# GNN and mixture layer on one core: edge products as two fp32r products of weighted rows, in lots of four edge tiles

## The reference

```python
# _layernorm: no gain, no bias, eps 1e-5
support = _layernorm(x) @ W
x = x + segment_sum(support[src] * edge_weight[:, None], dst, 12500) + b
# the experts, on h = _layernorm(x); one sample, so one routing for all tokens
w = softmax(mean(h) @ Wr + br)                 # capped by capacity, softmax again, top 2, softmax
y = sum over the two chosen e: w_e * (gelu(h @ W1[e] + b1[e]) @ W2[e] + b2[e])
x = x + layernorm(y + h, gamma, beta)
```

## Time and profile before

| | us |
|---|---|
| median of three runs | 2384.93 |
| the profiled execution: its own time | 2382.08 |
| the profiled execution: span | 2380.3 |
| PE busy / PEld busy | 2210.0 / 1729.8 |
| DVE busy | 1025.3 |
| ACT busy | 1193.3 |
| POOL busy | 1516.3 |
| first gather, last gather (start) | 11.27, 1973.68 |

### The profile page before, as it was taken

How to read it: one execution, slowest core, us unless ns; L and a number is a source line. 1 busy time by engine, 2 the same in 40 slices (tenths; PEclk the granted TensorE clock), 3 DMA queues, 4 the chain that set the end, 5 groups by cost and what they waited for, 6 DMA issues and landing times. The chain is left out here.

```text
span 2380.3 us, 41661 instructions
## 1 busy us (share of the span) xinstructions
PE 2210.0 (93%) x9949; PEld 1729.8 (73%) x9950; DVE 1025.3 (43%) x2952; ACT 1193.3 (50%) x3202; POOL 1516.3 (64%) x1594
## 2 busy tenths in 40 slices
PE   2488999899999999999999999999998999999998
PEld 1366777677776767777777777777776777999998
DVE  7893233232332233232332322232222235899989
ACT  3577666665655555544534343322324125565664
POOL 6777777777777777777777777777777771000100
PEclk9999999999999999999999999999999999999999
DMA  9955667666666655566656656556566554242431
GB/s 369 336 168 157 205 202 241 187 189 180 180 187 181 181 176 175 178 179 197 186 178 180 189 179 187 175 182 190 169 194 172 186 161 141 95 140 95 136 98 54
DMA packets 226740, 425.79 MB, mean 179 GB/s; under 512 B 36675, under 2 KB 134774, under 8 KB 226600
## 3 DMA queue, kind: packets, MB, share of 16 engines
q0 software_dynamic: 75008, 204.90, 29.5%
q1 hardware_dynamic: 151160, 217.12, 28.0%
q10 hardware_dynamic: 432, 2.40, 0.3%
HBM read 341.53 MB, written 82.75 MB: 178 GB/s over the span
## 5 line engine op out<-in xcount | busy, mean ns | idle before, releaser
L588 POOL DMA_INDIRECT G<-xr_d,SRC x1467 | 1391.8, 949 | 447.0 <-issue 298.6
L1072 DVE TENSOR_SCALAR OH<-CST,DL,WR 128x128 f32<-128x128 f32 x1563 | 567.4, 370 | 1272.3 <-PE ps L1463 1151.0
L1463 PE MATMUL ps<-G,OH 128*128 x3126 | 739.8, 389 | 78.6 <-DVE OH L1072 57.8
L1463 PEld LDWEIGHTS ps<-G,OH 128*128 128x128 f32 x3126 | 597.0, 194 | 224.1 <-issue 143.0
L1446 PE MATMUL ps<-W2u,H 128*128 128x256 f32 x1920 | 430.9, 382 | 6.9 <-issue 6.3
L1435 PE MATMUL ps<-YU,W1u 128*128 128x512 f32 (+1 forms) x1024 | 426.1, 568 | 9.6 <-ACT H L767 8.4
L1446 PEld LDWEIGHTS ps<-W2u,H 128*128 128x128 f32 x1920 | 363.1, 191 | 69.8 <-issue 20.9
L1435 PEld LDWEIGHTS ps<-YU,W1u 128*128 128x128 f32 x1024 | 194.8, 191 | 206.1 <-issue 184.7
L775 ACT ACTIVATE YE<-ps 128x512 f32<-128x512 f32 (+1 forms) x128 | 72.6, 569 | 442.3 <-PE ps L1446 442.1
L767 ACT ACTIVATE H<-ps,b1a 128x512 f32<-128x512 f32 (+1 forms) x256 | 168.5, 660 | 225.9 <-PE ps L1435 225.6
L602 POOL TENSOR_TENSOR ZR<-ZV,mhalf 128x4 f32<-128x4 f32 (+1 forms) x24 | 30.5, 1272 | 348.6 <-DVE ZV L1256 348.6
(11 more groups left out here) (221 smaller groups left out, 2302.1 us busy)
## 6 DMA issues: line engine op xcount, KB each, us to landing
W1u<-in_W SPq DMA_DIRECT2D x64, 512.0 KB
W2u<-in_W SPq DMA_DIRECT2D x64, 512.0 KB, 4.7
y_d<-YE SPq DMA_DIRECT2D x56, 512.0 KB, 5.7
G<-xr_d,SRC POOLq DMA_INDIRECT x1467
x_d<-X SPq DMA_DIRECT2D x98, 128.0 KB
yt_d<-YT SPq DMA_DIRECT2D x98, 128.0 KB
XR<-in_x SPq DMA_DIRECT2D x97, 128.0 KB, 3.1
XL<-x_d SPq DMA_DIRECT2D x24, 512.0 KB, 4.9
```

What stands on the lines that cost most here:

```text
L588: e.indirect_dma_start(out=G[0:rows(s), held(s), :], out_offset=None, in_=x if s < FRESH else xr_d, in_offset=bass.IndirectOffsetOnAxis(ap ...
L1072: e.tensor_scalar(OH[:, s % OHR, :], iota, DL[:, s:s + 1], WR[:, s + 1:s + 2], ALU.is_equal, ALU.mult).then_inc(s_oh, 1)
L1463: e.matmul(ps[:, 0, 0:D], OH[:, r, :], Gf[:, bass.ds(g + r * D, D)], start=False, stop=True, skip_group_check=True).then_inc(s_main, 1)
```

## The change

The edge product is no longer fp32 with the weight in the 128x128 matrix. The matrix is now a plain one-hot in fp32r; the gathered rows are multiplied by their weights on VectorE, and the weighted rows are split there into a high part rounded to fp32r and a low part, the rest. TensorE does two fp32r products for each edge tile, with the same one-hot. All of this goes in lots of four edge tiles (LOT = 4): four VectorE operations for a lot (parts). The first 96 tiles stay fp32 on TensorE, with rows weighted on VectorE one tile at a time (weighted) and one-hots made four at a time (one_hots). The last three tiles go singly (last_parts).

The ring of gathered rows shrinks from 72 to 36 slots, and a slot is free when VectorE has divided its rows, not when TensorE has multiplied them. The new ring of divided rows GW and the ring of one-hots OH have 16 places each. Gathers wait once a lot instead of every time, and share one semaphore per lot. The test for events, the end of a node tile and the repeated products go by four edge tiles instead of two: begin has four tiles (eight fp32r matmuls, in the first 96 tiles four fp32 products). ScalarE makes four matrices for it instead of two, without the weights. The experts' part is unchanged.

```diff
-RING, GS, OHR = 64, 16, 8
+HELD, GS, LOT, RING = 36, 9, 4, 16
+OWN, TURN = 8, NE - 44
-HELD = RING + OHR
 # gpsimd
-                if s >= HELD:
-                    e.wait_ge(s_main, s - RING + 3)
...
-                if s >= GS:
-                    e.wait_ge(gat[s % GS], 16 * (s // GS))
+                if s >= HELD and s % LOT == 0:
+                    e.wait_ge(s_gw, before(s) + LOT)
+                if s >= GS * LOT and s % LOT == 0:
+                    e.wait_ge(gat[s // LOT % GS], 16 * LOT * (s // (LOT * GS)))
 # scalar
             def match(t):
-                for k in range(2):
-                    step(e.activation(OHT[:, 0, k, :], iota, ACT.Abs, bias=XND[:, k:k + 1]))
-                step(e.activation(OHT[:, 1, :, :], OHT[:, 0, :, :], ACT.Relu, bias=ones[:, 0:1], scale=-1.0))
+                for k in range(LOT):
+                    step(e.activation(OHT[:, k, :], iota, ACT.Abs, bias=XND[:, k:k + 1]))
+                e.activation(OHX[:, :, :], OHT[:, :, :], ACT.Relu, bias=ones[:, 0:1], scale=-1.0).then_inc(s_ohx, 1)
             def copy(v, t):
-                for k in range(2):
-                    e.activation(OHX[:, k, :], OHT[:, 1, k, :], ACT.Copy, scale=WR[:, bass.ds(odd + k, 1)]).then_inc(s_ohx, 1)
 # vector
-                if s >= OHR:
-                    e.wait_ge(s_main, s - OHR + 1)
-                e.tensor_scalar(OH[:, s % OHR, :], iota, DL[:, s:s + 1], WR[:, s + 1:s + 2], ALU.is_equal, ALU.mult).then_inc(s_oh, 1)
+            def one_hots(s, m):
+                if s >= RING:
+                    e.wait_ge(s_main, s - RING + m + 1)
+                e.tensor_tensor(out=OH[:, s % RING:s % RING + m, :], in0=iota.unsqueeze(1).to_broadcast([P, m, P]),
+                                in1=DL[:, s:s + m].unsqueeze(2).to_broadcast([P, m, P]), op=ALU.is_equal).then_inc(s_oh, m)
+            def weighted(s):
+                if s % LOT == 0:
+                    one_hots(s, LOT)
...
+                e.tensor_scalar(GF[:, s % RING, 0, :], G[:, held(s), :], WR[:, s + 1:s + 2], None, ALU.mult).then_inc(s_gw, 1)
+            def parts(s):
+                g, r = slice(held(s), held(s) + LOT), slice(s % RING, s % RING + LOT)
+                e.wait_ge(gat[s // LOT % GS], 16 * LOT * (s // (LOT * GS) + 1))
+                e.tensor_tensor(out=G[:, g, :], in0=G[:, g, :], in1=WR[:, s + 1:s + LOT + 1].unsqueeze(2).to_broadcast([P, LOT, D]), op=ALU.mult).then_inc(s_gm, 1)
+                one_hots(s, LOT)
+                e.wait_ge(s_gm, (s - FRESH) // LOT + 1)
+                e.tensor_copy(GW[:, r, 0, :], G[:, g, :]).then_inc(s_gh, 1)
+                e.wait_ge(s_oh, s + LOT)
+                e.wait_ge(s_gh, (s - FRESH) // LOT + 1)
+                e.tensor_tensor(out=GW[:, r, 1, :], in0=G[:, g, :], in1=GW[:, r, 0, :].bitcast(f32), op=ALU.subtract).then_inc(s_gw, LOT)
+            def last_parts(s):
+                if s == NE - LOT:
+                    one_hots(s, LOT - 1)
...
+                e.tensor_scalar(GW[:, s % RING, 0, :], G[:, held(s), :], WR[:, s + 1:s + 2], None, ALU.mult).then_inc(s_gh, 1)
+                e.scalar_tensor_tensor(out=GW[:, s % RING, 1, :], in0=G[:, held(s), :], scalar=WR[:, s + 1:s + 2], in1=GW[:, s % RING, 0, :].bitcast(f32), op0=ALU.mult, op1=ALU.subtract).then_inc(s_gw, 1)
 # tensor
-                e.matmul(ps[:, 0, 0:D], OH[:, r, :], Gf[:, bass.ds(g + r * D, D)], start=False, stop=True, skip_group_check=True).then_inc(s_main, 1)
+            def edge(r, fresh):
+                if fresh:
+                    ins = e.matmul(ps[:, 0, 0:D], OH[:, r, :].bitcast(f32), GF[:, r, 0, :], start=False, stop=True, skip_group_check=True)
+                else:
+                    for h in range(2):
+                        ins = e.matmul(ps[:, 0, 0:D], OH[:, r, :], GW[:, r, h, :], start=False, stop=True, skip_group_check=True)
+                ins.then_inc(s_main, 1)
```

More of the change, by code:

```diff
@@ L35, in held, with before @@
 def held(s):
-    return s if s < OHR else OHR + (s - OHR) % RING
+    return s % HELD if s < TURN else OWN + (s - TURN) % (HELD - OWN)
+def before(s):
+    return s - (HELD if s < TURN + HELD - OWN else HELD - OWN)
 def xtiles(g):
@@ L110 @@
 assert 2 * NEV <= 512
-assert NE % OHR == 4 and EDGES <= (NE - 1) * P
+assert NE % RING == 12 and FRESH % RING == 0 and EDGES <= (NE - 1) * P
+assert TURN % HELD == OWN and all(held(s) == held(before(s)) for s in range(HELD, NE))
 def gnn_ffn(nc, x, dflat, srct, dstt, wt, W, b, Wr, br, W1, b1t, W2, b2, gamma, beta, cst, iota_e, evt, out):
@@ L1084, in fresh @@
                     for f in range(4 * s - 48, 4 * s - 44):
-                        one_hot(f)
+                        weighted(f)
                 if s >= 20:
-                    one_hot(s - 12)
+                    weighted(s - 12)
                 stats_end(s)
@@ L1104, in _ @@
                 newton_steps(FRESH // 8 - 1, range(4 * j, 4 * j + 4))
-                one_hot(FRESH - 12 + j)
-            for s in range(FRESH - 8, NE - 1):
-                one_hot(s)
+                weighted(FRESH - 12 + j)
+            for s in range(FRESH - 8, FRESH):
+                weighted(s)
+            for s in range(FRESH, NE - LOT, LOT):
+                parts(s)
+            for s in range(NE - LOT, NE - 1):
+                last_parts(s)
             rn = 0
@@ L1487, in event, with slots @@
                         with e.If(now == END):
[L1488 to L1503 removed]
+                            begin(e.snap(v_r, min_val=1, max_val=FINAL), r, fresh)
+            def slots(first, last, fresh):
+                with e.Fori(first // RING, last // RING) as i:
+                    a = e.snap(i * RING)
+                    e.reg_mov(rel, e.snap(due) - a)
+                    for r in range(RING):
+                        if r % LOT == 0:
+                            e.wait_ge(s_gw, a + (r + LOT))
+                        edge(r, fresh)
+                        if r % LOT == LOT - 1:
+                            event(a, r, fresh)
+            slots(0, FRESH, True)
+            slots(FRESH, NE // RING * RING, False)
             def last_across():
```

120 lines of the change are left out of this document (58 added, 62 removed).

## The result

The changed kernel takes **2606.56 us** (median of 3 runs, 2599.27 to 2611.31) against 2384.93: a ratio of 1.0925 (95% interval 1.0883 to 1.0967), slower by 222 us. The profiled execution took 2606.56 us, its span is 2604.6.

The account below looks back on a forecast made before the run. POOL's gather stream was taken as the bound. 2382.08 (profiled execution) + 126 (steady holds) + 19 (first 96 tiles) + 1.5 (tail) = 2528.6 us, median 2531, stated as 2530; forecast 2470 to 2695 (chance 0.60), wider range 2425 to 2720.

Parts of the forecast that it names:

- The bound: Edge stage: POOL issues a gather every 1.25 us without waiting for others, and this stream sets the stage's end.
- TensorE's saving: Edge products: some 350 us less PE work at most, all becoming idle time, worth nothing.
- rival 3: Edge stage: TensorE is the bound, 2125 us or part of it; or POOL's gap shrinks with fewer waits, 2300; chance 0.05.
- The cause of the holds: Gathers wait at a point 0.13 us after their start until a two-SBUF-input or fast single-input VectorE operation ends.
- Rival 1: Gathers beside VectorE: little contention, 10 to 60 us of holds, sum 2441, range 2415 to 2470 us; chance 0.20.
- The steady holds: Gathers from the 129th on: 90% of lots at +0.24 us, 10% at +1.4, together +126 us.
- The worked-out lot: One lot followed from its multiply: holds of 0.09, 0.13 and 0.02 us, period 5.24 us where it was 5.00.
- rival 2: Heavy contention: random phases, casts stopping later parts, or compare starting before a waiting gather; 2695 to 2905 us; chance 0.15.
- This costs nothing by itself: Start: the 37th gather's wait for the fourth weighted tile, behind 85 us, was charged nothing.
- The tail: Behind the last gather: VectorE's remaining lot and single tiles add 1.5 us (0.5 to 3).
- the first tiles: First 96 tiles: the 129th gather's lot waits for weighted tile 96 near 195 us, +19 us (12 to 25).
- The chance of slower: Whole kernel: slower by over 0.2% has chance 0.94, within that 0.01, faster 0.05.

Follow-up runs that it names:

- experiment 8: The changed kernel with the low product of every edge tile behind the 96th done twice: 2610.67 us.
- experiment 1: The changed kernel with one input of compare, multiply and subtract taken from a constant in PSUM instead of SBUF, rows not weighted: 2453.76 us.
- experiment 11: The kernel before plus a 128x1024 multiply with two SBUF inputs per four edge tiles, its output unread: 3070.89 us, beside 3220.10 for the kernel before on that chip.
- experiment 3: The changed kernel with the compare of each lot behind tile 96 done twice: 2862.61 us.
- experiment 5: The changed kernel with all four VectorE operations of a lot each cut into four single-tile ones, same arithmetic: 2548.82 us.
- experiment 7: The changed kernel with the compare's row of column numbers kept in PSUM, same arithmetic: 2586.42 us.
- experiment 12: The kernel before plus a cast of 128x1024 per four edge tiles, its output unread: 3187.61 us, beside 3220.10 for the kernel before on that chip.
- experiment 4: The kernel before with a ring of 40 gathered tiles instead of 72, nothing else: 2431.70 us.
- experiment 10: The changed kernel without separate multiply, compares in single tiles, 44 places for gathered rows instead of 36 and 12 for weighted instead of 16: 2560.18 us.

## Why the prediction was right, and where its steps were off

**The bound: right.** POOL's stream of gathers sets the end, before and after; its gap stayed at 0.30 us (447.0 us for 1467, both times) although three of four gathers lost their waits. TensorE's saving was worth nothing (experiment 8), so rival 3 falls on both its counts.

**The cause of the holds: right.** From the 130th on every long gather of the changed kernel ends 0.82 us behind a VectorE operation, and taking the second SBUF inputs away shortens the gathers by 104 of their 127 added ns (experiment 1). With the Trainium skill (SBUF — State Buffer, "Who interferes with whom") it goes as with the trace of before: its rule that a cast in a two-port mode holds GpSimd agrees (24.6 us here), its inference that tensor_tensor leaves descriptor generation alone does not (multiply and subtract, 140.8 us; and 200.9 in experiment 11). Rival 1, which followed from it, would have been 2441.

**The steady holds: the mechanism right, the size too small.** The term was +126 us; it measured 178.5, 0.50 us a lot in place of 0.35. The worked-out lot was nearly exact in its length: the four gathers from 227.23 on, which the multiply hardly touches, take 5.20 us (the fourth starts at 231.07 and lasts 1.06, and 0.30 follow), for which I had 5.24. This is in part luck. I had taken 0.55 us from the end of a gather to VectorE's start, out of the earlier trace rows, by pairing the matrix of 1972.67 with the gather that ends at 1972.12. That matrix waited for the gather before it, which started at 1969.92. Timeline of the kernel before:
```profile
1969.92 0.95 POOL L588 DMA_INDIRECT G<-xr_d,SRC  x1 [0.30 <-PE ps L1463]
```
It ended at 1970.87, 1.80 us before the matrix. The error is 1.25 us, just one period of the gathers, so the multiply falls at the same place beside a gather and the sum stands. The split doesn't: I had 0.09, 0.13 and 0.02 us for multiply, cast and subtract, and these four gathers show 0.01, 0.07 and 0.11. Over the whole stretch the cast and the subtract make 0.24 of the 0.50. What failed is that 90% of the lots lie so. The multiply held a gather in 230 of some 359 lots, 0.34 us on average, and I put that on TensorE, which releases VectorE at a random time behind a unit. TensorE released it for 1.9 us in all. It is the landing. In the 334 lots in which VectorE waited for it, the multiply started 1.90 us behind the end of the lot's fourth gather in the median, but in one of four over 2.50 and in one of twenty over 4.2. Of the 136 such lots at 1.8 to 1.9 us half have a held gather beside the multiply, by 0.07 us on average over the lots; of the 59 at 2.1 to 2.8 nearly all, by 0.59. The 138 lots over 2.0 us have 62 of the multiply's 79 us. (In 24 more lots VectorE itself was still at the lot before.) Why a landing takes longer no experiment tried, but the DMA records of the same trace show what goes with it: in the 1.8 us behind the fourth gather the 16 DMA engines are busy with the other transfers (queue q1) for 1% of the time where the multiply starts within 1.85 us (116 lots), and for 62% where it takes over 3.5 us (31 lots).

Of rival 2's grounds the phases came in part. The second, that a cast also stops the later part of a gather, is real: it shows in experiments 1, 3, 5, 7 and 12 (41, 175, 23, 18 and 125 gathers that end 0.12 us behind a cast). In the changed kernel no gather is held so, and so it adds nothing there. The third, that VectorE starts its next operation before a waiting gather gets in, shows between short casts (experiment 5), and not between the operations of the changed kernel's lots.

**"This costs nothing by itself": wrong, the step that failed.** I saw that the 37th gather would wait until 83 us, and charged nothing, since weighted tile 96 near 195 would set the 129th gather anyway. Tile 96 was weighted at 188.1, and the 129th gather started at 213.3. I had compared VectorE's new end with the old time of that gather, and not asked when the gathers get there once they have lost 25 us: at 1.25 us each, behind a VectorE that needs 1.10, they can't make them up. The term was +19 and measured 37.1: 29.0 lost at the ring (experiment 4 shows a short ring losing 36 with the old arithmetic; the 8 places of experiment 10 win back 8) and 8.1 of holds beside the backlog, in which VectorE has no idle time and the gathers take 1.44 and 1.66 us.

**The tail: +1.5 predicted, 8.8 measured.** From the last gather's start to AS it is 7.92 us (2189.20 to 2197.12) where it was 3.63, and another 4.5 come after. Timeline of the changed kernel behind the last gather:
```profile
2189.20 0.90 POOL L596 DMA_INDIRECT G<-xr_d,SRC  x1 [0.30 <-issue]
...
2190.74 1.23 DVE L1095 TENSOR_TENSOR GW<-G,GW 128x1024 fp32r<-128x1024 f32 x1
...
2194.43 0.48 DVE L1104 SCALAR_TENSOR_TENSOR GW<-G,WR,GW 128x256 fp32r<-128x256 f32 x1
...
2197.12 0.38 ACT L841 ACTIVATE AS<-ps 128x256 f32<-128x256 f32 x1 [55.10 <-PE ps L1509]
...
2198.91 2.07 PE L1563 MATMUL ps<-Wsb,AT 128*128 128x256 f32 x4
```
The last whole lot ends at 2191.97, 2.8 us behind the last gather's start, and the three single tiles at 2194.91. Then the four matmuls with Wsb take 2.07 us; before they took 1.13. The stretches of the changed kernel show the clock beside it (busy time of each engine, then granted clock, DMA share, GB/s):
```profile
1200.00:1500.00 300.00, 242.82 (x1096) 188.12 (x1095) 208.27 (x221) 112.34 (x304) 232.95 (x221) 0.86 0.55 165
...
2150.00:2200.00 50.00, 22.80 (x86) 19.44 (x87) 35.19 (x44) 0.77 (x2) 30.84 (x31) 0.50 0.32 92
```
Between 2150 and 2200 TensorE is busy for 23 of 50 us, in short pieces between waits, and its clock is at 0.50, the lower level (1.2 GHz), when the routing begins. In the kernel before it was at 1.00 there. TensorE's idle time, which I booked at zero, has this price; no experiment separates the clock's part of the 4.5 us.

**The sum** came out at 2530 and not at 2607 because the steady term was 52 us short, the first tiles 18 and the tail 7: all of the 78 us between 2528.6 and the profiled 2606.56. The chance of slower, and the range, held.

## What to carry to other kernels

When an engine is one long stream of equal instructions, price a change by what it does to that instruction and to the stream's start, not by the busy time that it saves elsewhere; here 112 us less TensorE work came with 187 us of longer gathers. Two-input SBUF operations and fast casts on VectorE stop GpSimd's gathers until they end. What helped here was a two-input operation cut into short ones, or one input taken from PSUM; casts cut into pieces back to back did not help. A buffer made smaller costs where it is full for the first time, and the loss stays whenever what follows has no faster pace than before: ask of every stall "who can make it up?".

## What the runs showed that I had not expected

- Four casts of 128x256 back to back (0.89 us together) hold a gather until the fourth has ended, though four multiplies by tensor_scalar (1.33 us together) let it in: 173 gathers were held for 93 us by the casts, and 31 for under 2 us by the multiplies.
- A cast holds a gather at two places: at its point (the gather ends 0.82 us behind the cast) and in its later part (0.12 us behind). A two-input operation does the first alone, in every trace.
- The granted clock follows the idle time inside the edge stage: 0.86 to 0.88 between 195 and 1500 us in the changed kernel, 0.91 and 0.93 in two of the same stretches with a third product, 0.95 to 1.00 before.
- A gather delays VectorE too: the cast of 128x1024 took 0.81 us where it started in a gather's last part (223.93), and 0.69 in the backlog's lots (208.35).
- On one chip the kernel before took 3220 us. It has stayed unexplained. In the traces of experiments 11 and 12, from that chip, TensorE waits 184 and 205 us before the repeated products of begin, where it waited 36 in the trace of before.
